# Attention and feed-forward on one core: GpSimd's two maxima over the partitions taken apart, input loads before stack loads, the last batch's fillers moved

## The chip, the cores and the metric

The kernel runs on one core of one Trainium2 chip. The metric is the device time of one execution in microseconds (us), lower is better. Engines are TensorE (PE; its weight loads are PEld), VectorE (DVE), ScalarE (ACT), GpSimd (POOL) and SyncE (SP), which issues the DMAs.

## The reference, cut to what matters

```python
# x: (16, 1024, 256), heads of 16 x 16, hidden 768, weights of the feed-forward part are integers
q, k, v = heads(x @ Wq.T + bq), heads(x @ Wk.T + bk), heads(x @ Wv.T + bv)
attn = softmax(einsum('hbnd,hbmd->hbnm', k, q) / 16)
x = layernorm(x + merge(einsum('hbnm,hbmd->hbnd', attn, v)) @ Wo.T + bo)
gate, up = x @ w_gate.T / 127, x @ w_up.T / 127
x = layernorm(x + (silu(gate) * up) @ w_down.T / 127)
```

## The kernel before, in words

The 16 batches run one after the other. A batch is 64 **steps**: 4 groups of 4 heads, two halves of 512 columns, 8 tiles of 128 tokens. In a step TensorE writes two pairs of score tiles (`score`), ScalarE takes their exponentials into `probs` (line 599), and TensorE multiplies them by the values (`products`) and sums in one PSUM bank, `ACC`. Products of two steps are issued together in every even step, for the two steps before it. Each 8 steps make a **segment**: VectorE then transposes the bank into `flipped` (`take_segment`, line 850), which gives the bank free; the products that begin the next segment wait for that.

The remaining work of a batch is done as **fillers** between the scores of odd steps, three PSUM banks in a ring: the projections `qk`, `norm` and `v` of the batch that follows, and `out`, `x1T`, `gate`, `up` and `down` of the batch before it. The class `Plan` gives each filler a due step on VectorE and GpSimd from a list of blocks, one block for two steps; both engines then run their work strictly in the order of those due steps. In batches 1 to 14 the blocks are `FULL_BLOCKS`, which the change leaves alone; the first batch uses `PRE_PLAN`, the last `POST_BLOCKS`.

What the change touches:

- `find_xmax` (VectorE, four reductions over `x_pre` at steps XMAX to XMAX + 3): the largest input of the batch after next. GpSimd takes it over the partitions (`reduce_xmax`, lines 479 and 481). `find_scale` (VectorE, before the first item due after step SCALE) waits for that.
- `reduce_norms` (GpSimd, lines 495 and 497): the same for the norms of the queries and keys, once VectorE has done filler `norm` 1 (line 734). `decide` (VectorE, step DECIDE) waits for it, TensorE waits for the flag at step RELOAD.
- GpSimd's other work: `square` (line 489) after each `qk`, `split_low` (line 510) after each `up`, `make_rstd` (line 503) after each `out` and `down`, and `add_bias` (line 523) on the loaded residual, `x_res`.
- Two waits of VectorE on GpSimd: `normalise` (line 795) waits for `rstd`, and filler `up` j waits before it writes `h32` (line 765) for `split_low` of `up` j - 2:

```python
                    if j >= 2:

                        dve.wait_ge(h_lo_ready, 2 * HCHUNKS * post + j - 1)
```

- SyncE's queue, in order, at the change of batch: the results of the batch before last (`store_result`, after the last `normalise`), the load of `x_res`, the wait for the last scores of the batch before, 12 loads of `qstack` and `kstack` for group 1 (`load_stack`), the load of `x_pre`.

Order of VectorE's items in a full batch (due step): take 0 (8.55), out 0 to 3 (10, 12, 14, 16), x1T and qk in turns (18 to 25), gate and up j at about 26 + 2j, norm 1 (36.0), gate 7 and up 7 (40.1, 40.45), take 4 (40.55), v 0 and 1 (50, 52), down 0 and its normalise (54, 54.9), v 2 (56), take 6 (56.55), v 3 and scaling of x (58), down 1 to 3 (60 to 64). GpSimd's: out 3 (16.0), square of qk 4 (19.15), up 4 (34.65), up 5 (36.65), up 9 (44.65), up 10 and 11, down 0 (54.0).

After batch 15 its own out, x1T, gate, up and down run alone: the **tail**. Its first addition (line 745) needs the residual of batch 15, loaded and with its bias.

Of the kernel before, what the change touches and what calls it, by code (L numbers as in the profile page):

```python
# [63 lines left out]
UNITS = 2 * STEPS  # L64
# [11 lines left out]
def some(kind, *js):  # L76
    return [(kind, j) for j in js]


def gate_up(*gs):  # L80
    return [(kind, g) for g in gs for kind in ("gate", "up")]
# [10 lines left out]
def halves(kind, j):  # L92
# [1 line left out]
    return [[(kind, j, 0, half)], [(kind, j, half, 2 * half)]]  # L94


POST_BLOCKS = ([[]] + [some("out", j) for j in range(4)] + [some("x1T", j) for j in range(4)]
               + [gate_up(g) for g in range(2 * HCHUNKS)]
               + [half for j in range(4) for half in halves("down", j)])
ONLY_POST = [item for item in FULL if item[0] in POST]  # L100
# [7 lines left out]


PREPARE = 8  # L110
XMAX, SCALE = 18, 54
POOL_REDUCE = 46
DECIDE, RELOAD = 50, 52
ESC_LOAD = 58

INTS, WMAX, WIDE = 22, 28, 56
POOL_WMAX = 40
PRE_STEPS = 52

# [74 lines left out]
PREPARES = [PER_GROUP * g + PREPARE for g in range(GROUPS)]  # L194
FULL_PLAN, PRE_PLAN, POST_PLAN = Plan(FULL_BLOCKS, PREPARES), Plan(evenly(ONLY_PRE, PRE_STEPS), PREPARES), Plan(POST_BLOCKS, PREPARES[:-1])
LOADS = 4 * len(Q_PARTS)
# [6 lines left out]
def build(nc, x, xt, Wq_t, bq, Wk_t, bk, Wv_t, bv, Wo_t, bo, gate_t, up_t, down_t, out):  # L203
    ctx = ExitStack()
    with ctx:  # L205
# [3 lines left out]
        def sem(name):  # L209
# [14 lines left out]
        scaled = sb("scaled", [P, HALVES, HALF])  # L224
# [62 lines left out]
        x1T = [ffn16[:, 4 * H + i * X1:4 * H + (i + 1) * X1].rearrange("p (c n) -> p c n", c=CHUNKS)  # L287
               for i in range(2)]
# [33 lines left out]
        scores_ready, probs_ready, pv_done = sem("scores_ready"), sem("probs_ready"), sem("pv_done")  # L322
# [12 lines left out]
        @block.sync  # L335
        def _(sp):
            sp.dma_start(x_pre[:, :, :], xt_v[0]).then_inc(x_pre_loaded, 16)
            for tile, w in ((WqT, Wq_t), (WkT, Wk_t)):
                sp.dma_start(tile[:, :, :], w.rearrange("(c p) n -> p c n", p=P)).then_inc(qk_loaded, 16)
            for i, w in enumerate((gate_t, up_t, down_t)):  # L340
                sp.dma_start(ints[:, 1536 * i:1536 * (i + 1)].bitcast(I32).rearrange("p (c n) -> p c n", c=w.shape[0] // P),
                             w.rearrange("(c p) n -> p c n", p=P)).then_inc(ints_loaded, 16)

            def store_parts(n, idx):


                sp.wait_ge(squares_ready, QK * n + 2 * idx + 2)
                sp.dma_start(parts_dram[n, idx].rearrange("j p n -> p j n"), parts[:, idx % 2, :, :]
                             ).then_inc(parts_stored[idx % 2], 16)

            def load_stack(b, g):
                slot, c, odd = g % 2, g // 2, g % 2

                for t, (stack, which) in enumerate(((qstack, Q_PARTS), (kstack, K_PARTS))):
                    src = parts_dram[b, 2 * c + t]
                    for half in range(2):
                        at = ROW_TILE * half
                        for r, part in enumerate(which):
                            sp.dma_start(stack[at + r * HEAD_DIM:at + (r + 1) * HEAD_DIM, slot, :, :],
                                         src[part].rearrange("(h d) n -> d h n", d=HEAD_DIM)[:, odd + 2 * half::4, :]  # L360
                                         ).then_inc(stack_loaded[slot], 16)

            def load_shift(b, g):
                sp.wait_ge(shift_ready, GROUPS * b + g + 1)
                n = PAIRS * TILES
                for half in range(2):
                    for r in range(SHIFT_ROWS):
                        at = ROW_TILE * half + ROWS + r
                        sp.dma_start(kstack[at:at + 1, g % 2, :, :].rearrange("o h (t n) -> o (h t) n", t=TILES),
                                     shift_parts[n * half:n * (half + 1), r, :]).then_inc(shift_loaded, 16)  # L370

            def store_result(b):
                for s in range(2):

                    sp.wait_ge(y_ready, 4 * b + 2 * (s + 1))
                    sp.dma_start(out_v[b][:, TPH * s:TPH * (s + 1), :], x_res[:, TPH * s:TPH * (s + 1), :]
                                 ).then_inc(out_stored, 16)


            sp.wait_ge(x_scaled, 2)  # L380
            sp.dma_start(x_pre[:, :, :], xt_v[1]).then_inc(x_pre_loaded, 16)
            store_parts(0, 0)
            store_parts(0, 1)
            for s in range(2):
                sp.wait_ge(parts_stored[s], 16)
            load_stack(0, 0)
            store_parts(0, 2)
            store_parts(0, 3)
            load_shift(0, 0)

            def batch(b, first, last, ahead=2):
                if not first:
                    sp.wait_ge(scores_ready, UNITS * b)
                load_stack(b, 1)
                if not last:

                    sp.wait_ge(x_scaled, 2 * b + 4)
                    sp.dma_start(x_pre[:, :, :], xt_v[ahead:BATCHES][b]).then_inc(x_pre_loaded, 16)
                if not first and not last:
                    store_parts(b + 1, 0)  # L400
                    store_parts(b + 1, 1)
                load_shift(b, 1)
                if first:
                    store_parts(b + 1, 0)

                sp.wait_ge(scores_ready, UNITS * b + 2 * PER_GROUP)
                if first:
                    for s in range(2):
                        sp.wait_ge(parts_stored[s], 32)
                load_stack(b, 2)  # L410
                if first:
                    store_parts(b + 1, 1)
                elif not last:
                    store_parts(b + 1, 2)
                    store_parts(b + 1, 3)
                load_shift(b, 2)
                sp.wait_ge(scores_ready, UNITS * b + 4 * PER_GROUP)
                load_stack(b, 3)
                if first:
                    store_parts(b + 1, 2)  # L420
                load_shift(b, 3)
                if first:
                    store_parts(b + 1, 3)
                if not last:
                    sp.wait_ge(scores_ready, UNITS * b + 6 * PER_GROUP)

                    for s in range(2):
                        sp.wait_ge(parts_stored[s], 32 * (b + 2))
                    load_stack(b + 1, 0)
                    load_shift(b + 1, 0)  # L430
                if first:
                    sp.dma_start(x_res[:, :, :], x_v[0]).then_inc(x_res_loaded, 16)
                else:
                    store_result(b - 1)

                    sp.wait_ge(out_stored, 32 * b)
                    sp.dma_start(x_res[:, :, :], x_v[1:BATCHES][b - 1]).then_inc(x_res_loaded, 16)

            batch(0, True, False)
            with sp.Fori(1, BATCHES - 2) as b:  # L440
                batch(b, False, False)

            batch(BATCHES - 2, False, False, ahead=1)
            batch(BATCHES - 1, False, True)
            store_result(BATCHES - 1)

            sp.wait_ge(out_stored, 32 * BATCHES)
# [3 lines left out]
        def _(pool):  # L451
# [24 lines left out]
            def reduce_xmax(n):  # L476

                pool.wait_ge(xmax_ready, n)
                nc.gpsimd.tensor_tensor(xmax_safe[:, :], xmax[:, :], margin[:, 0:1], ALU.mult)
                pool.drain()  # L480
                nc.gpsimd.partition_all_reduce(xmax_all[:, :], xmax_safe[:, :], P, RMAX).then_inc(xmax_reduced, 1)
# [44 lines left out]

            def batch(b, first, last):
                plan = PRE_PLAN if first else POST_PLAN if last else FULL_PLAN
                reduced, seen = last, not first
                for at, kind, j, n in plan.pool + [(STEPS, None, 0, 0)]:  # L530
                    if at >= POOL_WMAX and not seen:
                        pool.wait_ge(wmax_ready, 1)
                        nc.gpsimd.partition_all_reduce(wmax_all[:, :], wmax[:, :], P, RMAX).then_inc(wmax_reduced, 1)
                        seen = True
                    if at >= POOL_REDUCE and not reduced:
                        reduce_norms(b + 1)
                        reduce_xmax(b + 2)
                        reduced = True
                    if kind:
                        take(kind, j, n, base(b), b - 1)  # L540
                add_bias(b)
# [711 lines left out]
```

## Time and profile before

| what | value |
|---|---|
| median of 3 runs | 2720.08 us (2719.48 to 2722.92) |
| the profiled execution, its own time | 2718.36 us |
| its span | 2716.3 us |
| mean granted clock of TensorE | 0.985 |
| PE busy | 2606.4 us, 96% |
| ACT busy | 2131.7 us, 78% |
| DVE busy | 1285.6 us, 47% |
| POOL busy | 538.6 us, 20% |

The profile is of one execution. Busy time is the time in which an engine executes something, not its waits; the time of the execution is 2.06 us above the span, which lies between the first and last instruction of the trace.

### The profile page before, as it was taken

Reading aid. Unit: us, or ns where it says so; the run is one execution under the profiler, and the core shown is the slowest. Engines: PE = TensorE matmul, PEld = TensorE weight load, DVE = VectorE, ACT = ScalarE, POOL = GpSimd, SP = SyncE. Lnnn points to the kernel's source line nnn. Section 1 sums busy time; section 2 is a strip of 40 time slices with the busy share of each in tenths; the row PEclk is TensorE's granted clock in tenths of the full one; section 3 lists DMA queues with packets and bytes.
Section 4 is the critical chain, followed back from the end, with each engine's and each line's share of the span. In section 5 each row is a group of like instructions: output and inputs, shape, how many; then the busy total and the mean of one; then the engine's idle time right before and its main releaser. Section 6 shows DMA issues by size and latency. Waiting matters only on the chain. (4 is left out here: it accounts for less than half of the span.)

```text
span 2716.3 us, 47000 instructions
## 1 busy us (share of the span) xinstructions
PE 2606.4 (96%) x17294; PEld 936.0 (34%) x17294; DVE 1285.6 (47%) x2812; ACT 2131.7 (78%) x2370; POOL 538.6 (20%) x542
## 2 busy tenths in 40 slices
PE   6879999999999999999999999999999999999897
PEld 2223333333324333333333323333333333334234
DVE  3324445454453544445454553545445454453447
ACT  2878878788787878878788787878878788787781
POOL 2101122121222212122121121212122121221113
PEclk9999999999999999999999999999999999999998
DMA  4112021120212102121120202102121030201000
GB/s 154 49 39 70 26 79 38 48 71 22 87 34 74 48 22 86 33 75 41 30 85 25 87 29 73 55 14 94 33 75 40 22 95 25 87 29 56 18 27 29
DMA packets 81742, 144.08 MB, mean 53 GB/s; under 512 B 27584, under 2 KB 29504, under 8 KB 79424
## 3 DMA queue, kind: packets, MB, share of 16 engines
q1 hardware_dynamic: 79968, 139.81, 16.5%
q8 instruction: 172, 2.82, 0.4%
q14 instruction: 98, 0.80, 0.1%
q10 hardware_dynamic: 1504, 0.66, 0.1%
HBM read 88.48 MB, written 50.33 MB: 51 GB/s over the span
## 5 line engine op out<-in xcount | busy, mean ns | idle before, releaser
L599 ACT ACTIVATE probs<-psum 128x1024 f32<-128x1024 f32 x2048 | 1983.7, 1023 | 497.3 <-PE psum L1010 497.1
L1010 PE MATMUL psum<-probs,v 128*32 128x512 f32 x8192 | 1007.2, 610 | 39.9 <-DVE flipped L850 39.3
L1010 PE MATMUL psum<-kstack,qstack 51*128 51x512 f16 x4096 | 633.4, 384 | 31.9 <-ACT probs L599 28.0
L1010 PEld LDWEIGHTS psum<-probs,v 128*32 128x32 f32 x8192 | 217.3, 110 | 555.0 <-issue 522.1
L1010 PEld LDWEIGHTS psum<-kstack,qstack 51*128 51x128 f16 x4096 | 134.3, 93 | 724.0 <-ACT probs L599 647.2
L510 POOL TENSOR_TENSOR ffn<-h,ffn 128x512 f16<-128x512 f32 x192 | 221.4, 1155 | 678.1 <-DVE ffn L769 578.5
L724 DVE SCALAR_TENSOR_TENSOR tanh_out<-tanh_out,psum 128x512 f32<-128x512 f32 x192 | 131.3, 684 | 335.4 <-ACT tanh_out L580 335.4
L715 DVE SCALAR_TENSOR_TENSOR parts<-psum,scales,parts 128x512 f16<-128x512 f32 x128 | 94.9, 741 | 269.1 <-ACT parts L571 268.9
L489 POOL TENSOR_TENSOR squares<-parts 128x512 bf16<-128x512 f16 x128 | 131.9, 1038 | 433.0 <-DVE parts L715 433.0
L503 POOL TENSOR_TENSOR rstd<-vareps,minus_half 128x2 f32<-128x2 f32 x128 | 89.6, 700 | 584.3 <-DVE vareps L788 584.3
L1010 PE MATMUL psum<-ffn,gateT 128*128 128x512 f16 x768 | 200.4, 384 | 0.3 <-DVE ffn L757 0.3
L1010 PE MATMUL psum<-ffn,upT 128*128 128x512 f16 x768 | 198.1, 380 | 0.5
L1010 PE MATMUL psum<-downT,ffn 128*128 128x256 bf16 x1536 | 180.1, 274 | 0.0
L795 DVE TENSOR_SCALAR x_res<-x_res,meanvar,rstd 128x256 f32<-128x256 f32 x256 | 93.5, 408 | 172.2 <-POOL rstd L503 172.2
L850 DVE STREAM_TRANSPOSE flipped<-psum 128x512 f32<-128x512 f32 x128 | 91.4, 714 | 159.2 <-PE psum L1010 159.2
L1010 PEld LDWEIGHTS psum<-downT,ffn 128*128 128x128 f16 x1536 | 145.6, 98 | 46.8 <-issue 30.0
L765 DVE SCALAR_TENSOR_TENSOR h<-tanh_out,h_scale,psum 128x512 f32<-128x512 f32 x192 | 143.5, 748 | 22.4 <-DVE tanh_out L724 1.5
L580 ACT ACTIVATE tanh_out<-psum 128x512 f32<-128x512 f32 x192 | 116.3, 606 | 35.2 <-PE psum L1010 24.4
L749 DVE SCALAR_TENSOR_TENSOR x_res<-psum,down_scale,x_res 128x512 f32<-128x512 f32 x64 | 48.0, 750 | 180.0 <-PE psum L1010 180.0
L1010 PE MATMUL psum<-WvT,xT 128*128 128x256 f32 x512 | 130.2, 396 | 2.2 <-issue 2.2
L1010 PE MATMUL psum<-xT,WqT 128*128 128x512 f32 x256 | 127.5, 620 | 2.6 <-DVE xT L775 2.6
L1010 PE MATMUL psum<-WoT,outT 128*128 128x256 f32 x512 | 126.8, 391 | 0.0
(102 smaller groups left out, 1529.9 us busy)
## 6 DMA issues: line engine op xcount, KB each, us to landing
parts_dram<-parts SPq DMA_DIRECT2D x64, 512.0 KB, 2.8
qstack<-parts_dram SPq DMA_DIRECT2D x384, 64.0 KB, 2.1
kstack<-parts_dram SPq DMA_DIRECT2D x384, 64.0 KB, 2.1
x_pre<-in_x_t SPq DMA_DIRECT2D x17, 1024.0 KB, 5.1
x_res<-in_L_attn_x SPq DMA_DIRECT2D x16, 1024.0 KB, 5.2
out<-x_res SPq DMA_DIRECT2D x32, 512.0 KB, 2.7
kstack<-shift_parts SPq DMA_DIRECT2D x384, 4.0 KB, 1.7
ffn<-in_L_ffn_w_gate SPq DMA_DIRECT2D x1, 768.0 KB, 9.7
```

The lines of the kernel that those rows point to most:

```text
L489: nc.gpsimd.tensor_tensor(squares[:, idx, cols], parts[:, idx % 2, 0, cols], parts[:, idx % 2, 0, cols], ALU.mult).then_inc(squares_ready, 1)
L503: nc.gpsimd.tensor_tensor(rstd[:, tiles], vareps[:, tiles], minus_half[:, tiles], ALU.pow).then_inc(rstd_ready, 1)
L510: nc.gpsimd.tensor_tensor(hT[hf][1][:, hc, :], h32[:, g % 2, :], hT[hf][0][:, hc, :], ALU.subtract).then_inc(h_lo_ready, 1)
L580: nc.scalar.activation(tanh_out[:, g % 2, :], bank[RING + (start + n) % RINGS], ACT.Tanh, scale=0.5 * W_SCALE).then_inc(tanh_ready, 1)
L599: nc.scalar.activation(probs[:, (STEPS * b + k) % SLOTS, 2 * pr:2 * pr + 2, :], scores[pr], ACT.Exp, scale=score_scale[par]).then_inc(prob ...
L715: nc.vector.scalar_tensor_tensor(out=parts[:, idx % 2, 1, cols], in0=o, scalar=scale[:, BIAS + idx:BIAS + idx + 1], in1=parts[:, idx % 2, ...
L724: nc.vector.scalar_tensor_tensor(out=gated, in0=gated, scalar=1.0, in1=o, op0=ALU.add, op1=ALU.mult).then_inc(ring_free, 1)
L749: nc.vector.scalar_tensor_tensor(out=tiles, in0=o, scalar=down_scale[:, 0:1], in1=tiles, op0=ALU.mult, op1=ALU.add).then_inc(ring_free, 1)
L765: nc.vector.scalar_tensor_tensor(out=h32[:, j % 2, :], in0=tanh_out[:, j % 2, :], scalar=h_scale[:, 0:1], in1=o, op0=ALU.mult, op1=ALU.mul ...
L795: ins = nc.vector.tensor_scalar(x_res[:, t, :], x_res[:, t, :], meanvar[:, t, 0:1], rstd[:, t:t + 1], ALU.subtract, ALU.mult)
L850: nc.vector.transpose(flipped[:, hf, :], bank[ACC]).then_inc(acc_free, 1)
L1010: return nc.tensor.matmul(o, lhsT, rhs, start=start, stop=stop)
```

## The change

GpSimd's two reductions stood together, between the splits of up 9 and up 10. Now the one of the inputs comes after the `rstd` of out 3, the one of the norms before the split of up 5. VectorE's part moves with them: the reductions over `x_pre` from steps 18 to 21 to steps 6 to 9, `find_scale` from 54 to 22, `decide` from 50 to 44, the reload of the flag from 52 to 50. SyncE issues the load of `x_pre` ahead of the wait and the 12 stack loads. In the last batch the out fillers come three blocks later, x1T in two blocks instead of four, and gate, up and down two blocks later.

```diff
-POST_BLOCKS = ([[]] + [some("out", j) for j in range(4)] + [some("x1T", j) for j in range(4)]
+POST_BLOCKS = ([[], [], [], []] + [some("out", j) for j in range(4)] + [[]] + [some("x1T", 0, 1), some("x1T", 2, 3)]
                 + [gate_up(g) for g in range(2 * HCHUNKS)]
                 + [half for j in range(4) for half in halves("down", j)])
...
-XMAX, SCALE = 18, 54
-POOL_REDUCE = 46
-DECIDE, RELOAD = 50, 52
+XMAX, SCALE = 6, 22
+POOL_XMAX, POOL_NORMS = 16.2, 36.3
+DECIDE, RELOAD = 44, 50
...
-INTS, WMAX, WIDE = 22, 28, 56
+INTS, WMAX, WIDE = 24, 28, 56
...
             def batch(b, first, last, ahead=2):
+                if first:
+                    load_stack(b, 1)
+                if not last:
+
+                    sp.wait_ge(x_scaled, 2 * b + 4)
+                    sp.dma_start(x_pre[:, :, :], xt_v[ahead:BATCHES][b]).then_inc(x_pre_loaded, 16)
                 if not first:
                     sp.wait_ge(scores_ready, UNITS * b)
-                load_stack(b, 1)
-                if not last:
-
-                    sp.wait_ge(x_scaled, 2 * b + 4)
-                    sp.dma_start(x_pre[:, :, :], xt_v[ahead:BATCHES][b]).then_inc(x_pre_loaded, 16)
+                    load_stack(b, 1)
...
-                reduced, seen = last, not first
+                scaled, reduced, seen = last, last, not first
...
-                    if at >= POOL_REDUCE and not reduced:
+                    if at >= POOL_XMAX and not scaled:
+                        reduce_xmax(b + 2)
+                        scaled = True
+                    if at >= POOL_NORMS and not reduced:
                         reduce_norms(b + 1)
-                        reduce_xmax(b + 2)
                         reduced = True
```

## Rows read from the trace of the kernel before

**Rows 1.** Waits of PE: who was waited for, total us, times, longest

```profile
PE psum L1010 <- DVE flipped L850: 39.3, 15, 4.3
```

**Rows 2.** Timeline of DVE, batch 2: start, us, instruction, [idle before it, its releaser]

```profile
509.69 0.73 DVE L795 TENSOR_SCALAR x_res<-x_res,meanvar,rstd 128x256 f32<-128x256 f32 x2 [6.74 <-POOL rstd L503]
...
512.38 0.70 DVE L850 STREAM_TRANSPOSE flipped<-psum 128x512 f32<-128x512 f32 x1
```

**Rows 3.** Timeline of POOL, batch 2, the two reductions

```profile
479.56 0.20 POOL L495 TENSOR_TENSOR norm_safe<-norm,margin 128x2 f32<-128x2 f32 x1
485.83 0.37 POOL L497 PARTITION_ALL_REDUCE norm_all<-norm_safe  x1 [6.07 <-issue]
493.12 0.18 POOL L479 TENSOR_TENSOR xmax_safe<-xmax,margin 128x1 f32<-128x1 f32 x1 [6.92 <-issue]
...
506.69 2.27 POOL L510 TENSOR_TENSOR ffn<-h,ffn 128x512 f16<-128x512 f32 x2 [6.81 <-issue]
508.93 0.73 POOL L503 TENSOR_TENSOR rstd<-vareps,minus_half 128x2 f32<-128x2 f32 x1
```

**Rows 4.** Timeline of PE, four places

```profile
204.13 0.61 PE L1010 MATMUL psum<-kstack,qstack 51*128 51x512 f16 x4 [3.08 <-issue]
...
471.56 1.92 PE L1010 MATMUL psum<-probs,v 128*32 128x512 f32 x16
...
513.23 3.50 PE L1010 MATMUL psum<-probs,v 128*32 128x512 f32 x16 [2.23 <-DVE flipped L850]
...
2479.00 3.20 PE L1010 MATMUL psum<-probs,v 128*32 128x512 f32 x16 [2.93 <-DVE flipped L850]
```

**Rows 5.** Windows: stretch, its length, busy time by engine, granted clock, DMA

```profile
514.00:515.00 1.00, 1.00 (x12) 0.41 (x8) 0.92 (x3) 0.00 (x0) 0.00 (x0) 0.50 0.08 20
```

**Rows 6.** Timeline of DVE, batch 2, steps 36 to 41

```profile
455.96 0.15 DVE L734 TENSOR_REDUCE norm<-norms 64x1 f32<-64x2 f32 x1
...
467.58 0.75 DVE L765 SCALAR_TENSOR_TENSOR h<-tanh_out,h_scale,psum 128x512 f32<-128x512 f32 x1
...
468.79 0.72 DVE L850 STREAM_TRANSPOSE flipped<-psum 128x512 f32<-128x512 f32 x1
```

**Rows 7.** Timelines of SP's queue, DVE and PE, start of batch 3

```profile
538.11 0.35 SPq L437 DMA_DIRECT2D x_res<-in_L_attn_x  x1
...
545.13 0.40 SPq L398 DMA_DIRECT2D x_pre<-in_x_t  x1
...
553.21 0.72 DVE L850 STREAM_TRANSPOSE flipped<-psum 128x512 f32<-128x512 f32 x1 [3.64 <-PE psum L1010]
...
556.08 1.92 PE L1010 MATMUL psum<-probs,v 128*32 128x512 f32 x16
```

**Rows 8.** Timelines of POOL and DVE, batch 3, steps 18 to 23

```profile
579.15 1.04 POOL L489 TENSOR_TENSOR squares<-parts 128x512 bf16<-128x512 f16 x1 [6.08 <-DVE parts L715]
...
588.79 0.75 DVE L715 SCALAR_TENSOR_TENSOR parts<-psum,scales,parts 128x512 f16<-128x512 f32 x1 [2.29 <-ACT parts L571]
```

**Rows 9.** Timelines of DVE and PE, last batch, steps 4 to 14

```profile
2516.07 0.69 DVE L745 TENSOR_TENSOR x_res<-psum,x_res 128x512 f32<-128x512 f32 x1 [12.94 <-POOL x_res L523]
...
2521.10 0.61 PE L1010 MATMUL psum<-kstack,qstack 51*128 51x512 f16 x4
2526.05 3.64 PE L1010 MATMUL psum<-probs,v 128*32 128x512 f32 x16 [4.35 <-DVE flipped L850]
...
2531.36 0.39 PE L1010 MATMUL psum<-kstack,qstack 51*128 51x512 f16 x2
...
2535.96 0.39 PE L1010 MATMUL psum<-kstack,qstack 51*128 51x512 f16 x2 [0.32 <-ACT probs L599]
```

**Rows 10.** Timelines of DVE, SP's queue and POOL, into the tail

```profile
2646.39 0.34 SPq L437 DMA_DIRECT2D x_res<-in_L_attn_x  x1
...
2651.14 4.54 POOL L523 TENSOR_TENSOR x_res<-x_res,bo_all 128x2048 f32<-128x2048 f32 x1 [8.23 <-DMA x_res<-in_L_attn_x]
...
2658.66 0.65 DVE L745 TENSOR_TENSOR x_res<-psum,x_res 128x512 f32<-128x512 f32 x1
```

More of the change, by code:

```diff
@@ L391, in batch @@
             def batch(b, first, last, ahead=2):
-                if not first:
-                    sp.wait_ge(scores_ready, UNITS * b)
-                load_stack(b, 1)
+                if first:
+                    load_stack(b, 1)
                 if not last:
@@ L398, in batch @@
                     sp.dma_start(x_pre[:, :, :], xt_v[ahead:BATCHES][b]).then_inc(x_pre_loaded, 16)
+                if not first:
+                    sp.wait_ge(scores_ready, UNITS * b)
+                    load_stack(b, 1)
                 if not first and not last:
```

## The prediction, made before the changed kernel was run

> **What bounds the kernel now.** I read the page first: PE is busy 96% of the span, so the question is where its few idle stretches are. The waits of PE name one that repeats: 39.3 us in 15 waits for VectorE's transpose `flipped`, the longest 4.3 [rows 1]. The timeline of PE places them: one in each of the batches 1 to 14, at the products that open the segment of step 56, and a 15th in the last batch. Without the 4.35 of the last [rows 9] the fourteen make 34.95 us, 2.50 each; in batch 2 it is 2.23 [rows 4].
>
> The timeline of VectorE says why the transpose is late. In batch 2 it starts at 512.38, right behind `normalise` of down 0, which sat 6.74 us waiting for GpSimd's `rstd` [rows 2]. The timeline of GpSimd says why that is late: it begins the norms' reduction at 479.56 and the splits of up 10 and 11 only at 506.69; `rstd` follows at 508.93 [rows 3]. The two reductions hold GpSimd for 27.13 us, though the instructions themselves take 0.2 and 0.4 each; the rest is "issue", 6.07 us ahead of the PARTITION_ALL_REDUCE, 6.92 and 6.81 behind one.
>
> A stall costs more than its length. The 16 products behind it take 3.50 us, where 16 take 1.92 otherwise [rows 4], and the granted clock there is 0.50 [rows 5], the lower level of 1.2 GHz. So a stall costs its 2.50 and 1.58 of clock. All fourteen are of this kind, with the products behind them slow (batch 14: 2.93 and 3.20), but a gap is not always enough: the 3.08 us at 204.13 were followed by scores at 0.61, full speed [rows 4].
>
> **What the change removes.** With nothing but `rstd` on GpSimd at step 54, `normalise` follows its input at once and `find_scale` is not there any more. The transpose then starts when its products are done, three steps of filler ahead of the need. Fourteen stalls go: 14 x (2.50 + 1.58) = 57 us.
>
> **What it adds at step 36.** One reduction is half of the pair: from 479.56 to 493.12 it is 13.56, from 493.12 to 506.69 it is 13.57 [rows 3]. It now begins when norm 1 is done, at 455.96 + 0.15 = 456.11 [rows 6], plus 0.10 to hand over (an estimate; the matmul of [rows 4] follows the end of its transpose by 0.15). Behind it waits the split of up 5, which can start at 456.21 + 13.57 = 469.78 and takes half of 2.27 [rows 3]: it ends at 470.92. Up 6 doesn't need it, up 7 does: it writes the half of `h32` that the split of up 5 reads. So VectorE, which wrote up 7 at 467.58, can't before 470.95, 3.37 later. Right behind up 7 in VectorE's order stands take 4: 468.79 [rows 6] becomes 472.16. PE resumed 0.85 after the start of the late transpose (513.23 - 512.38, [rows 2, 4]), so here at 473.01; it wants the bank at 471.56 [rows 4]. That is a new stall of 1.45 us in each full batch. Take 1.5: 14 x 1.5 = 21 us back. Gate 9 comes some 2.4 us after those products, and up 7 and gate 8 have freed their banks by then, so nothing more is late.
>
> The bounds. From below 0, if the way back of 6.92 is not paid (rival 2). From above: both ways at 6.92 make the trip 0.57 + 13.84 = 14.4, the stall 2.3 and the loss 32. To this may come the clock. The clock at a stall of 1.5 is in no row. The nearest are 2.23, where it fell, and 3.08, where it did not; the new gap is shorter than either and stands right behind a full pair of gate and up and before a full group of products. So I take no fall, and keep 14 x 1.58 = 22 us for the range.
>
> The Trainium skill (GPSIMD Engine Reference, 2.1 Instruction dispatch) says that the first call of a freshly loaded GpSimd kernel pays about 6 us of loading that no instruction shows. The trace agrees with 6.07 ahead of the reduction [rows 3]. The page prices no way back, and by it alone the trip would be some 6.6 us; the rows show 6.92 and 6.81 behind the reductions, and the sum goes by the rows.
>
> **What moves at nothing, and its cover.** The inputs' reduction now begins behind `rstd` of out 3, at about 573.1, and gives GpSimd back 13.57 later, at 586.7. The square of qk 4, at 579.15 [rows 8], and that of qk 5 wait for it; only the store of those parts hangs on them, and SyncE's next store waits for the square of qk 7 at about 595 anyway. No wait of VectorE or PE is on a square before step 31. `find_scale` (some 1.4 us) comes ahead of qk 6, where VectorE has 2.29 idle [rows 8]; its maximum is there since 580. The reductions over `x_pre` move to steps 6 to 9. The load of `x_pre` is issued behind that of `x_res`, at 538.5 instead of 545.13 [rows 7]. A load of this size lands after 4.75 us (2646.39 to 2651.14, [rows 10]); two in a row make at most 9.5, so by 548. VectorE's first reduction then delays qk 2 by a us at most. Take 0 starts at 553.21 when its products are done, and PE wants it at 556.08, so it may start up to 555.2 [rows 7]. The 12 stack loads fall behind by one load of 5 us; they are needed at step 16, some 25 us on. The first batch waits for the same things with more room.
>
> **The last batch.** Before, out 0 on VectorE waited 12.94 us for the residual, which delayed the transpose of segment 1 and stalled PE 4.35. The block from 2521.10 took 10.26 us, the next 4.60 [rows 9]: 5.7 us of stall and clock. With out 0 at step 9, at about 2517 to 2519, the residual is there: -5.7. The blocks without filler and those with x1T or half a down take the same 4.60, since ScalarE sets them, so spreading them differently costs nothing.
>
> But down 3 now ends two blocks, 9.2 us, nearer to the end, and a chain hangs on it: down 3 on VectorE, its norm, its store, the load of the residual (2646.39), the bias (2651.14, 4.54 long, done at 2655.68), the first addition of the tail (2658.66) [rows 10]. There were 3.0 us to spare. With 9.2 more the bias ends at 2664.9 and the tail starts 6.2 later, and all of it follows. +6.2, so the last batch gives back what it saves.
>
> **The sum**, against the profiled execution's 2718.36: -57 + 21 - 5.7 + 6.2 = -35.5, which gives 2682.9. The median stands 1.7 above that execution, so I predict 2684.5 us, 1.3% faster. Its own range: -2 to +11 for the length of the new stall, 5 either way for the last batch, where four blocks without filler now stand in a row and the clock may fall: 2676 to 2697.
>
> **Rivals.**
>
> 1. *The clock falls at the new stall too.* For it: it fell at all fourteen stalls, of 2.50 us on average. Against it: the 3.08 without a fall, and the shorter gap. 2684.5 + 22 = 2706.5, still 0.5% faster.
> 2. *The way back is not paid before a split.* A trip of 6.64 (0.20 + 6.07 + 0.37) ends at 462.9, the split of up 5 is done at 464, up 7 is not late: 2684.5 - 21 = 2663.5. This is also what the Trainium skill's page (the same section) gives if its 6 us are the whole price. Against it stand both ways back in [rows 3].
> 3. *The new stall is worth the old one.* A trip of 14.4 makes it 2.3, and with the clock 3.9 against 4.1: about 2718, no change. Only the tail and the last batch are left, and they cancel.
> 4. *Slower: `x_pre` is not there at step 6.* VectorE would stand before qk 2 and take 0, with about 2.2 us of work (two reductions, qk 2) between landing and transpose. PE is hit when the load lands after 553.0, and the kernel is slower than before when all fourteen batches lose another 2.5 us, that is from 555.5 on, 17 us after its issue, or from 554 with the clock. Landing at 556.0 it costs 14 x 3.0 = 42: 2726.5. Against it: at most 9.5 us for both loads.
>
> **How the numbers follow.** The forecast has 0.62, rival 1 0.16, rival 2 0.09, rival 3 0.05, rival 4 0.05, and 0.03 is left for something slower that I don't see. The range takes in the forecast's own and rival 1: 2669 to 2709; outside are rival 2 and the last three, 0.2 together. A measurement of this kernel tells 0.2% (5 us) from no change. Faster: the forecast and rivals 1 and 2, 0.87; same 0.05; slower 0.08.
>
> **What would show it.** In the waits of PE, fourteen for `flipped` of about 1.5 us (21 in all), now at take 4 and none at take 6. VectorE waits about 3.4 us for GpSimd's split before up 7 (line 765) in each full batch, and the 6.74 before `normalise` are gone. Granted clock 1.00 across step 42, or 0.50 by rival 1. No idle time of VectorE for `x_pre` of over 3 us before the reductions (line 683). No stall at 2521, and the tail's first addition preceded by a wait of some 6 us for the bias (line 523), which is later than the last transpose. I am wrong if the split after the reduction starts less than 10 us after `norm_safe`, or if there is another wait of PE that each batch repeats.

## The result, and the profile after

The changed kernel takes 2689.29 us, the median of 4 runs (2686.38 to 2696.20), the kernel before 2719.78 us (4 runs); the ratio is 0.9897, 95% interval 0.9883 to 0.9912. That is 1.0% faster, where 1.3% and 2684.5 us were forecast. The profiled execution took 2687.43 us, its span is 2685.4, the mean granted clock 0.993 instead of 0.985.

The waits of PE (who was waited for, total us, times, longest) answer to [rows 1]. One of the fourteen new stalls, 1.81 us at 1763.87, is put down to ScalarE:

```profile
PE psum L1014 <- ACT probs L603: 31.2, 53, 1.8
PE psum L1014 <- DVE flipped L854: 20.9, 13, 2.1
PE psum L1014 <- DVE absw L656: 15.5, 1, 15.5
PE psum L1014 <- issue: 6.8, 2, 4.7
```

So the stalls of the full batches add up to 22.7 us instead of 34.95. The place is the forecast one. The timelines of POOL, DVE and PE around step 40 of batch 2, in this order:

```profile
454.09 1.15 POOL L512 TENSOR_TENSOR ffn<-h,ffn 128x512 f16<-128x512 f32 x1 [3.94 <-DVE ffn L773]
456.00 0.20 POOL L497 TENSOR_TENSOR norm_safe<-norm,margin 128x2 f32<-128x2 f32 x1 [0.76 <-DVE norm L738]
462.21 0.37 POOL L499 PARTITION_ALL_REDUCE norm_all<-norm_safe  x1 [6.02 <-issue]
470.23 2.27 POOL L512 TENSOR_TENSOR ffn<-h,ffn 128x512 f16<-128x512 f32 x2 [7.65 <-issue]
...
471.51 0.75 DVE L769 SCALAR_TENSOR_TENSOR h<-tanh_out,h_scale,psum 128x512 f32<-128x512 f32 x1 [4.24 <-POOL ffn L512]
472.36 0.44 DVE L773 CAST ffn<-h 128x512 f16<-128x512 f32 x1
472.71 0.70 DVE L854 STREAM_TRANSPOSE flipped<-psum 128x512 f32<-128x512 f32 x1
...
473.56 1.92 PE L1014 MATMUL psum<-probs,v 128*32 128x512 f32 x16 [2.13 <-DVE flipped L854]
```

Read down, it is one chain: norm 1 releases the reduction, the reduction with its way back holds the split of up 5, this holds up 7 (line 769), behind it comes the transpose, and PE gets its bank 2.13 us late. This is the longest of the fourteen, because its trip (from `norm_safe` to the split) took 14.23 us; the others are 1.37 to 1.81. In all fourteen the stall is the trip less 12.1 us, to 0.01 (13.48 gives 1.37, 13.92 gives 1.81), and VectorE's wait ahead of up 7 is 3.48 to 4.24 us, where the forecast had 3.4; in half of them the profile puts that wait down to PE and not to the split. The 16 products behind it take 1.92, and the window of the same stretch shows the clock at its upper level; [rows 4, 5] showed 3.50 and 0.50:

```profile
474.00:475.00 1.00, 1.00 (x16) 0.30 (x8) 0.95 (x2) 0.00 (x0) 0.03 (x1) 1.00 0.03 4
```

At step 54, where VectorE waited 6.74 us for `rstd` [rows 2], it waits 0.85, and take 6 waits for PE and not the other way round (timeline of DVE):

```profile
505.81 0.74 DVE L799 TENSOR_SCALAR x_res<-x_res,meanvar,rstd 128x256 f32<-128x256 f32 x2 [0.85 <-POOL rstd L505]
...
510.07 0.72 DVE L854 STREAM_TRANSPOSE flipped<-psum 128x512 f32<-128x512 f32 x1 [1.67 <-PE psum L1014]
```

At the start of batch 3 the input is in time, with 1.44 us of wait ahead of a filler that isn't urgent, and take 0 waits for its products as in [rows 7]:

```profile
544.22 0.69 DVE L687 TENSOR_REDUCE xmax<-x_pre 128x1 f32<-128x512 f32 x1 [1.44 <-DMA x_pre<-in_x_t]
...
551.27 0.72 DVE L854 STREAM_TRANSPOSE flipped<-psum 128x512 f32<-128x512 f32 x1 [3.05 <-PE psum L1014]
```

In the last batch the stall of [rows 9] is gone, and in the tail the first addition waits for its bias, as forecast from [rows 10]. But two groups of products in blocks without filler are slow (3.52 here, 3.07 at 2508.86), and so is PE's start into the second half of its program, at 203.7. Timelines of PE and DVE:

```profile
203.71 1.04 PE L1014 MATMUL psum<-kstack,qstack 51*128 51x512 f16 x4 [4.66 <-issue]
...
2478.59 3.52 PE L1014 MATMUL psum<-probs,v 128*32 128x512 f32 x16
...
2628.43 0.69 DVE L749 TENSOR_TENSOR x_res<-psum,x_res 128x512 f32<-128x512 f32 x1 [7.27 <-POOL x_res L525]
```

Cut at the last transposes of batches 0, 14 and 15 and at VectorE's last instruction, the profiled executions divide like this (us; the forecast in the last line):

| | to the end of batch 0 | batches 1 to 14 | batch 15 | tail |
|---|---|---|---|---|
| before | 206.7 | 2294.1 | 155.6 | 56.5 |
| after | 208.4 | 2259.6 | 150.9 | 63.1 |
| difference | +1.7 | -34.5 | -4.7 | +6.7 |
| forecast | 0 | -36 | -5.7 | +6.2 |

### The profile page after: what moved, and what is told of

Same layout as the page of the kernel before. It is cut to its first block and busy times, and to the rows that moved or that the text cites. A ratio compares the mean times of both kernels' runs of the same rounds, so it can differ in the third digit from the quotient of the medians.

```text
span 2685.4 us, 47000 instructions
## 1 busy us (share of the span) xinstructions
PE 2585.0 (96%) x17294; PEld 934.6 (35%) x17294; DVE 1299.3 (48%) x2812; ACT 2131.6 (79%) x2370; POOL 539.7 (20%) x542
## 5 line engine op out<-in xcount | busy, mean ns | idle before, releaser
L1014 PE MATMUL psum<-probs,v 128*32 128x512 f32 x8192 | 989.6, 601 | 23.6 <-DVE flipped L854 20.9
```

Source lines behind the costliest of these rows:

```text
L1014: return nc.tensor.matmul(o, lhsT, rhs, start=start, stop=stop)
```

## The experiments

The same stretches for all kernels that were run, each a variant of the changed kernel:

| kernel | median us | ratio to before, interval | to the end of batch 0 | batches 1 to 14 | batch 15 | tail |
|---|---|---|---|---|---|---|
| norms' reduction one filler later | 2664.46 | 0.9800 (0.9777 to 0.9822) | 211.2 | 2236.3 | 149.4 | 64.0 |
| three buffers of h32 | 2660.11 | 0.9793 (0.9767 to 0.9819) | 208.6 | 2235.7 | 147.8 | 62.8 |
| stack loads ahead of x_pre | 2686.95 | 0.9882 (0.9856 to 0.9909) | 206.1 | 2261.0 | 150.9 | 64.2 |
| last batch as before | 2686.40 | 0.9888 (0.9862 to 0.9915) | 207.0 | 2262.7 | 152.3 | 55.6 |
| norms' reduction at 46 | 2663.42 | 0.9787 (0.9767 to 0.9806) | 210.3 | 2235.6 | 149.4 | 63.7 |
| that, and three empty blocks | 2657.44 | 0.9764 (0.9745 to 0.9782) | 209.9 | 2235.6 | 150.5 | 56.0 |
| that, and stack loads first | 2654.89 | 0.9761 (0.9743 to 0.9779) | 206.0 | 2236.0 | 149.5 | 55.2 |
| both reductions at 36.3 | 2899.94 (one) | | 209.3 | 2473.6 | 147.8 | 63.5 |
| inputs' reduction twice | 2752.67 (one) | | 212.8 | 2323.6 | 147.8 | 62.9 |

**The order of VectorE's items, not the trip.** The reduction of the norms one filler later:

```diff
-POOL_XMAX, POOL_NORMS = 16.2, 36.3
+POOL_XMAX, POOL_NORMS = 16.2, 38.3
```

> The changed kernel with the norms' reduction one filler later, between the splits of up 5 and up 6 (POOL_NORMS 38.3 for 36.3). My theory: the stall of the changed kernel (22.7 us in fourteen batches, 1.6 each) comes about only because up 7, which waits for the split of up 5, stands right ahead of take 4 on VectorE. One filler later it is up 8 that waits, some 2.6 us, and behind it comes no transpose for six steps. So PE has no wait for `flipped` in the full batches, VectorE's idle time before line 769 stays near 2.6 us a batch, the trip of GpSimd stays 13.5 to 14.2, and the time is 22 to 24 us below the changed kernel's: about 2666. Rival: the trip itself (its loading, whatever it does to the memory or to VectorE) slows the others, wherever it stands; then PE keeps about 20 us of waits, at other places, and the time stays near 2689.

The waits of PE and VectorE of this kernel; PE has none for `flipped`:

```profile
PE psum L1014 <- ACT probs L603: 29.5, 52, 0.9
PE psum L1014 <- DVE absw L656: 15.6, 1, 15.6
PE psum L1014 <- issue: 6.2, 2, 4.1
...
DVE h L769 <- POOL ffn L512: 38.4, 13, 3.4
```

VectorE still waits for GpSimd (3.0 us each in 13), only ahead of up 8, behind which no transpose stands. Batches 2 to 14 take 159.6 us each. By the medians it takes 25 us less than the changed kernel, where 22 to 24 were expected; the rival falls.

**The buffer that ties them.** The reduction stays at 36.3, `h32` gets a third buffer:

```diff
-        h32 = sb("h32", [P, 2, HALF])
+        h32 = sb("h32", [P, 3, HALF])
...
-                    if j >= 2:
+                    if j >= 3:
 
-                        dve.wait_ge(h_lo_ready, 2 * HCHUNKS * post + j - 1)
+                        dve.wait_ge(h_lo_ready, 2 * HCHUNKS * post + j - 2)
```

(and `j % 3`, `g % 3` where it is written and read)

> The changed kernel with three buffers of h32 instead of two, and the wait of up j for the split of up j - 3. GpSimd's trip stays at its place. My theory: up 7 no longer needs the split of up 5, up 8 needs it and it is there (about 471 in batch 2's time against 472), so VectorE's wait before line 769 falls from about 3.4 us a batch to near 0, the stall is gone, the time is 22 to 24 us below the changed kernel's: about 2666, as with the reduction one filler later. Rival (the trip itself slows the others): no change, about 2689.

```profile
PE psum L1014 <- ACT probs L603: 29.6, 52, 0.9
PE psum L1014 <- DVE absw L656: 15.7, 1, 15.7
PE psum L1014 <- issue: 7.1, 2, 4.9
PE psum L1017 <- DVE x_res L799: 5.1, 2, 3.4
```

The waits of PE are those of the run above, and VectorE waits for GpSimd's split no more. Both ways of cutting the chain give the same 2235.7 to 2236.3 us for batches 1 to 14; so the new stall was this chain. They are 23.9 us below the changed kernel's 2259.6; 22.7 of this are the stalls; where the other 1.2 lie was not traced. The stretch without a stall also prices the old one: 2294.1 - 2235.7 = 58.4 us, against 57 in the forecast.

**Doubling the trip.** Both reductions at 36.3:

```diff
-XMAX, SCALE = 6, 22
-POOL_XMAX, POOL_NORMS = 16.2, 36.3
+XMAX, SCALE = 6, 54
+POOL_XMAX, POOL_NORMS = 36.3, 36.3
```

> The changed kernel with both reductions at 36.3, one behind the other (find_scale back at step 54): the suspected cost doubled at the suspected place. My theory: every us of GpSimd's trip beyond the 12.1 or so that fit is a us of PE's wait at take 4. Both trips take 27.1 from the split of up 4, so the split of up 5 ends at about 28.3 us after norm 1 instead of 14.8, the stall grows from 1.6 to 14 to 15 us in each of fourteen batches, with a fall of the clock (some 1.6) behind each: 190 to 210 us above the changed kernel, about 2890. Rival: the stall is not set by the trip's length; then less than 2750.

Waits of PE, then the timelines of DVE and PE in batch 2:

```profile
PE psum L1014 <- DVE flipped L854: 206.1, 14, 15.3
...
499.80 0.75 DVE L769 SCALAR_TENSOR_TENSOR h<-tanh_out,h_scale,psum 128x512 f32<-128x512 f32 x1 [16.75 <-POOL ffn L512]
500.98 0.71 DVE L854 STREAM_TRANSPOSE flipped<-psum 128x512 f32<-128x512 f32 x1
...
501.83 2.79 PE L1014 MATMUL psum<-probs,v 128*32 128x512 f32 x12 [14.62 <-DVE flipped L854]
```

2899.94 us in one run, just above what I expected: 14.7 us a stall where 1.6 stood, and a granted clock of 0.50 behind all fourteen. Both trips together take 27.1 to 28.2 us, and here the stall is their length less 12.9 in all fourteen: beyond what fits, every us of the trip is a us of PE.

**The norms' reduction needn't move.**

```diff
-DECIDE, RELOAD = 44, 50
-POOL_XMAX, POOL_NORMS = 16.2, 36.3
+DECIDE, RELOAD = 50, 52
+POOL_XMAX, POOL_NORMS = 16.2, 46
```

> The changed kernel with the norms' reduction left where the kernel before has it (POOL_NORMS 46, DECIDE 50, RELOAD 52); only the inputs' reduction is moved. My theory: what frees VectorE at step 54 is that one trip instead of two stands behind up 9. It starts at about 23.5 us after norm 1 and is over 13.6 later, some 10 us before down 0's rstd is asked for; up 10 and 11 wait for splits that are done. So no wait of PE for `flipped` in the full batches, a batch takes 159.6 us, and the time is 22 to 27 us below the changed kernel's: 2662 to 2667. Rival: one trip there is still too long, VectorE still waits for rstd at down 0 or at up 11; then PE keeps a stall and the time lies between 2670 and 2700.

2663.42 us, batches of 159.6 us, no wait of PE for `flipped` (its largest are 29.5 for `probs` and 15.8 at the start, once). All that the change gains in the full batches comes from taking the inputs' reduction away from behind up 9; moving the norms' too costs back two fifths of it. The other way round, the norms' reduction moved and the inputs' left, was not run.

**Room at the other place.** The inputs' reduction done twice (an additional one, into a tile that nobody reads):

```diff
                     if at >= POOL_XMAX and not scaled:
+                        pool.wait_ge(xmax_ready, b + 2)
+                        nc.gpsimd.tensor_tensor(safe_more[:, :], xmax[:, :], margin[:, 0:1], ALU.mult)
+                        pool.drain()
+                        nc.gpsimd.partition_all_reduce(xmax_more[:, :], safe_more[:, :], P, RMAX)
+                        pool.drain()
                         reduce_xmax(b + 2)
```

> The changed kernel with the inputs' reduction at 16.2 done twice (the first into a tile that nobody reads): the other trip doubled. My theory: the place behind out 3 has room. The squares of qk 4 to 7 come up to 14 us later and VectorE's find_scale may wait some us ahead of qk 6, but no transpose stands close behind and the stack of the next group is loaded from older parts. At most 5 us above the changed kernel, 2687 to 2695. Rival: VectorE's wait for the maximum at step 22 (AR over at 593 instead of 580 in batch 3's time, find_scale due at 587) pushes qk 6 and 7, x1T and take 2 by 6 us and PE stalls each batch: 14 x 2 or more, 2715 or above.

Here my expectation failed and its rival held. Waits of DVE and PE, then their timelines in batch 3:

```profile
DVE scales L702 <- POOL xmax_all L485: 129.2, 15, 13.0
...
PE psum L1021 <- DVE parts L726: 29.4, 14, 2.8
PE psum L1021 <- DVE flipped L861: 24.9, 13, 2.4
...
604.96 0.27 DVE L702 TENSOR_SCALAR scales<-xmax_all,bound_slope 128x1 f32<-128x1 f32 x1 [8.78 <-POOL xmax_all L485]
...
607.14 1.04 PE L1021 MATMUL psum<-ffn,gateT 128*128 128x512 f16 x4 [2.58 <-DVE parts L726]
```

`find_scale` at step 22 is a wait too: VectorE stands 8.6 us for the maximum, the `qk` bank behind it comes free late, and PE stalls a second time in each batch. The time of 2752.67 us (one run) is 63 us above the changed kernel's. Batches 1 to 14 are 64 us longer: 29.4 of the second stalls, some 4 more at take 4, and for the most part of the rest the clock, which fell behind 14 of the 28 stalls. A trip at 16.2 costs nothing only while it is over before VectorE reaches step 22.

**The order of the loads.**

```diff
-                if first:
-                    load_stack(b, 1)
-                if not last:
-
-                    sp.wait_ge(x_scaled, 2 * b + 4)
-                    sp.dma_start(x_pre[:, :, :], xt_v[ahead:BATCHES][b]).then_inc(x_pre_loaded, 16)
                 if not first:
                     sp.wait_ge(scores_ready, UNITS * b)
-                    load_stack(b, 1)
+                load_stack(b, 1)
+                if not last:
+
+                    sp.wait_ge(x_scaled, 2 * b + 4)
+                    sp.dma_start(x_pre[:, :, :], xt_v[ahead:BATCHES][b]).then_inc(x_pre_loaded, 16)
```

> The changed kernel with SyncE's order of before: the 12 stack loads ahead of the load of x_pre. Theory A (mine): the input is still in time. The load is issued some 6.5 us later and lands about 16 us into the batch, VectorE's first reduction then holds qk 2 up by 1 to 2 us, take 0 is not late, and PE has no new wait. Besides, PE's gap where it enters the second half of its program (4.66 us of issue at 203.7 and a granted clock of 0.50 behind it, against 3.08 and 1.00 before) goes back to about 3.1, because no megabyte of x_pre stands in the DMA engines ahead of the fetch of its instructions: 2 to 4 us faster than the changed kernel, about 2686. Theory B: the earlier load is needed; take 0 is late in the fourteen full batches, by 1 us each or more with or without the clock, so 2700 or above. Theory C: the gap has nothing to do with the order and stays 4.7: 2689.

Waits of DVE and the timeline of PE:

```profile
DVE xmax L685 <- DMA x_pre<-in_x_t: 76.8, 13, 6.5
...
201.41 1.04 PE L1012 MATMUL psum<-kstack,qstack 51*128 51x512 f16 x4 [3.46 <-issue]
```

VectorE waits 77 us for the input instead of 32.5, and PE not at all for it: batches 1 to 14 take 2261.0 against 2259.6, the time can't be told from the changed kernel's. The input is in time in either order, so the forecast's fourth rival was far off and this part of the change gains nothing. The gap at the start of the second half did shrink from 4.66 to 3.46, but the clock behind it fell all the same (more on this gap in the next section).

**The last batch as before.** The line of `POST_BLOCKS` undone.

> The changed kernel with the blocks of the last batch as before. My theory: the tail starts when the last transpose is done and not 6.7 us later (line 749 has no wait for the bias), but out 0 waits for the residual again for about 13 us and the last batch has its stall of about 4.4 us with its clock, so it is 4.7 longer. Together 1 to 3 us faster than the changed kernel, about 2687. Rival: the late fillers of the last batch are what gains; without them it is 3 us or more slower.

Timelines of DVE and PE:

```profile
2483.51 0.69 DVE L749 TENSOR_TENSOR x_res<-psum,x_res 128x512 f32<-128x512 f32 x1 [11.48 <-POOL x_res L525]
...
2493.49 1.92 PE L1014 MATMUL psum<-probs,v 128*32 128x512 f32 x16 [2.90 <-DVE flipped L854]
```

2686.40 us: batch 15 is 1.5 longer, the tail 7.5 shorter. Batch 15 loses less than expected because the clock did not fall behind this 2.90 us stall. In this trace batches 1 to 14 took 3 us more (the clock fell at two of the stalls), which hides a part of the 6. The intervals of the two kernels overlap; the rival, 3 us slower, is not what came. By the stretches the late fillers cost 6 us more than they save, 3 of them by the falls of the clock in batch 15; by the medians the difference can't be told.

**Put together.** The reduction of the norms at 46, and in the last batch the outs one block earlier and no empty block behind them, so that down 3 ends where it did:

```diff
-POST_BLOCKS = ([[], [], [], []] + [some("out", j) for j in range(4)] + [[]] + [some("x1T", 0, 1), some("x1T", 2, 3)]
+POST_BLOCKS = ([[], [], []] + [some("out", j) for j in range(4)] + [some("x1T", 0, 1), some("x1T", 2, 3)]
```

> As the kernel with the norms' reduction at 46, and the last batch with three blocks without filler at its start instead of four, and none between out and x1T: down 3 ends at step 57 as in the kernel before, out 0 is at step 7. My theory: the residual of batch 14 is there some 19 us into the batch, which is where VectorE comes to out 0, so no stall (a wait of VectorE of up to 4 us ahead of take 0 costs PE nothing); the tail's first addition has its bias again, so the tail is 56.5 instead of 63 us after the last transpose. 6 to 8 us below the kernel with the reduction at 46 alone: about 2655, the best version. Rival: take 0, now behind out 0 on VectorE, is late and PE stalls 1 to 4 us with its clock in the last batch, which leaves 2 us or less of the gain.

The timeline of DVE at the start of the tail, where the first addition follows the last transpose by 2.3 us, not by 9.6 as in the changed kernel:

```profile
2595.95 0.72 DVE L854 STREAM_TRANSPOSE flipped<-psum 128x512 f32<-128x512 f32 x1 [12.64 <-PE psum L1014]
...
2598.22 0.65 DVE L749 TENSOR_TENSOR x_res<-psum,x_res 128x512 f32<-128x512 f32 x1
```

2657.44 us, 0.9764 of before, 6 us below the kernel with the reduction at 46 alone, as expected; batch 15 is 1.1 us longer (the clock fell at two groups of products, there at one), the tail 7.7 shorter. The same with the loads' old order:

> The version with the norms' reduction at 46 and three blocks without filler first in the last batch, with SyncE's order of before (stack loads ahead of the load of x_pre). With the order undone in the changed kernel, VectorE waited 77 us for x_pre instead of 33, and PE nothing. My theory: the same here, where no stall is left to hide anything: batches of 159.6 us, PE without a wait for `flipped`, the same time within 5 us, 2653 to 2662. What changes, if anything, is PE's gap where it enters the second half of its program (issue): 3.0 to 3.5 instead of 4.7. Rival: with no stall left, the later load shows as a wait of PE early in each batch, at take 0 or at the qk banks; then 0.5 us or more a batch, 2665 or above.

2654.89 us, ratio 0.9761: the same within the intervals, again with 77 us of VectorE's waits for the input (13 times) and none of PE's. This is the best version, with one edit less: 2.4% below the kernel before and, by the medians, 1.3% below the changed one. PE has no wait left that a full batch repeats: its 52 short waits for `probs` all lie in the first and the last batch.

## Why the prediction was right, point by point

- *What is removed.* Fourteen stalls with their clock, 57 us: 58.4, from the runs without any stall. Right.
- *The new stall.* The chain through the split of up 5, up 7 and take 4 is what the trace shows, and three runs confirm it: two that cut it at different links, one that doubled it. 1.5 us was the term, 1.62 the measured mean. The size was off because the fourteen trips took 13.73 us on average, up to 14.23, and the one that I read 13.57.
- *No fall of the clock at the new stall* (rival 1). None of the fourteen groups behind the stalls is slow. In two other runs the clock fell at one and two of fourteen such stalls, so the rival was wrong as a rule and right as a risk of a few us. That it fell nowhere in the profiled execution is in part luck: its stall of 2.13 kept the clock, two of 2.04 elsewhere did not. The four executions of the changed kernel have mean granted clocks of 0.990 to 0.993, the longest the lowest, but only one of them has a trace.
- *Rival 2, the way back not paid.* 7.65 us lie between the reduction and the split. The Trainium skill (GPSIMD Engine Reference, 2.1 Instruction dispatch) prices the way there, and the trace has it at 6.02; the way back is not in that section and is the longer of the two.
- *The moves at no cost.* Right, but the maximum for step 22 has little room: with 13.7 us more of trip VectorE waits 8.6, so some 5 us are to spare, and beyond them PE pays. That the input comes in time held with some 6 us to spare on top: with the old order its load is issued that much later (10.1 us behind the last transpose of a batch instead of 4.1), at no wait of PE.
- *The last batch.* -4.7 instead of -5.7, close only because two errors went opposite ways. The fall of the clock that the kernel before had in its last steps (16 products at 2649.57 took 3.11 us) is gone too, and fillers now stand there; without any fall batch 15 takes 147.8 in three of the runs, 7.8 below before. The falls in the empty blocks, 3 us here, I had only in the range.
- *The tail.* +6.7 against +6.2: the chain over the store, the load and the bias.
- *The range.* Its own range, 2676 to 2697, does not follow from its terms: -2 and -5 below and 11 and 5 above 2684.5 make 2677.5 to 2700.5. The measured 2689.29 lies in both.
- *Missing in the sum.* The first stretch is 1.7 us longer. PE's gap where it enters the second half of its program went from 3.08 to 4.66, and with the clock at 0.50 behind it the rest of the stretch took 4.67 instead of 2.53. Together that is 3.7 us, of which 2.0 don't show because PE reached the gap that much sooner (its last scores ahead of it began at 198.44, before at 200.44). Why it was sooner is not known; the first batch has other edits too (`INTS` from 22 to 24 among them), which no run undoes alone.

The length of the gap tells little. With `x_pre` first it is 4.1 to 5.1 us in six kernels but 3.0 and 1.5 in two, with the stacks first it is 2.9, 3.1 and 3.5. It depends on when PE arrives: in the kernel with the last batch as before PE came late, behind products that took 3.61 us, and its gap was 1.5. Timelines of SP's queue and PE there, then SP's queue in the changed kernel and in the one with the stack loads first:

```profile
193.81 0.58 SPq L434 DMA_DIRECT2D x_res<-in_L_attn_x  x1
...
197.58 3.61 PE L1014 MATMUL psum<-probs,v 128*32 128x512 f32 x16
...
203.23 0.71 PE L1014 MATMUL psum<-kstack,qstack 51*128 51x512 f16 x4 [1.50 <-ACT probs L603]
...
194.29 0.58 SPq L434 DMA_DIRECT2D x_res<-in_L_attn_x  x1
...
193.19 0.58 SPq L432 DMA_DIRECT2D x_res<-in_L_attn_x  x1
```

Counted from SyncE's issue of `x_res`, PE goes on 9.4 to 10.3 us later in all eight kernels with `x_pre` first (the two short gaps included, at 9.4 and 9.5), and 7.7 to 8.2 us later in all three with the stacks first. The first stretch agrees: 207.0 to 212.8 against 206.0 to 206.7. So the early load goes with a later restart of PE, of some 1.2 us or more, and does not help elsewhere. By what way it delays PE is not shown, and the clock falls behind the gap in either order.

The 4.8 us between the forecast and the median are these terms, +1.7 for the first stretch, +1.5 for the full batches, +1.0 for the last and +0.5 for the tail, which make up the 4.5 us by which the profiled execution (2687.43) missed its own sum (2682.9) within their rounding, and the median's distance from that execution, 1.9 instead of 1.7.

## What to carry to other kernels

When a long operation is moved on one engine, list who waits for the item behind it, and then what stands behind that waiter on its own engine: a wait of 4 us ahead of a buffer nobody needs yet costs nothing, the same wait one item ahead of a bank that the bound engine wants costs its whole length. Look for the slot where the chain ends in slack before taking a new one; here the old slot was free as soon as one of the two had left it. And at the end of a program the work that a load hangs on should be early, not late.

## What was not expected of the hardware

The way back from PARTITION_ALL_REDUCE to the next TENSOR_TENSOR on GpSimd, 6.6 to 7.9 us of "issue" over all runs, is longer than the way there, 5.8 to 6.6. Both come with 30 of the 32 reductions of the changed kernel, however often the same two kinds of work have taken turns before; behind the other two GpSimd waits longer than that for something else. And the length of a stall alone doesn't tell whether the granted clock falls. It fell to 0.50 behind all fourteen stalls of 2.14 to 2.93 us of the kernel before and behind none of the fourteen of 1.37 to 2.13 of the changed one. In the kernels with the stacks first and with the last batch as before it fell behind one of 1.93 and two of 2.04, and not behind one of 2.01, one of 2.17 and one of 2.90. With the inputs' reduction twice it fell behind 14 of 28, the shortest 1.79 us, and not behind some of 1.97 to 2.12. A fall costs about 1.6 us in a full batch: 58.4 us less 34.95 of stalls, over fourteen, is 1.7, and the row of batch 2 has 1.58.
